# Moving weight loads behind the first heads, halving four kinds of steps, and merging all engine orders anew in a two-layer decoder kernel

## The reference, cut to what matters

```python
x = ln(x + L0_attn(x))             # 16 heads of 16, rotary on q and k, softmax, projection + bias
x = ln(x + L0_xattn(x, ctx, ctx))  # mLSTM-like mixer: 8 heads of 32, q = x, k = v = ctx
                                   # gates from [x, ctx, ctx]; cumsum of log sigmoid, running max,
                                   # D = exp(F_i - F_j + i_j - max); C = q k^T * D / sqrt(32)
                                   # C v / max(|sum C|, exp(-max)), then a norm over each head's 32
x = ln(x + L0_ffn(x))              # int8-like activations, ternary weights:
                                   # h = relu(x Wg)^2 * (x Wu); out = quant(h) Wd
x = ln(x + L1_attn(x))             # 16 heads, no rotary
x = ln(x + L1_xattn(x, ctx, ctx))  # q from x, k and v from ctx, 16 heads, biases
x = ln(x + L1_ffn(x))              # relu(x W1 + b1) W2 + b2
```

## Time and profile before

| | before |
|---|---|
| median of 3 runs | 1883.49 us |
| the profiled execution | 1880.68 us |
| its span, first to last instruction | 1878.8 us |
| TensorE busy | 1595.6 us (85%) |
| VectorE busy | 1189.6 us (63%) |
| ScalarE busy | 965.7 us (51%) |
| GpSimd busy | 222.2 us (12%) |
| mean granted TensorE clock | 0.927 of full |

### The profile page before, as it was taken

How to read it: one execution, slowest core, us unless ns; L and a number is a source line. 1 busy time by engine, 2 the same in 40 slices (tenths; PEclk the granted TensorE clock), 3 DMA queues, 4 the chain that set the end, 5 groups by cost and what they waited for, 6 DMA issues and landing times.

```text
span 1878.8 us, 31464 instructions
## 1 busy us (share of the span) xinstructions
PE 1595.6 (85%) x12530; PEld 1019.0 (54%) x12546; DVE 1189.6 (63%) x2038; ACT 965.7 (51%) x1684; POOL 222.2 (12%) x201
## 2 busy tenths in 40 slices
PE   6388887888998878889999888789999987779888
PEld 4145554555665545455566445456556654546556
DVE  4866778546347777755645875865645677775452
ACT  2067464544554564545465565454556456544643
POOL 5101110010112110101011101100111100100000
PEclk9599998999999998899999988799999989979999
DMA  7600111213110102123111111031320120111200
GB/s 227 214 2 1 40 60 60 91 41 96 57 57 19 67 1 80 60 71 94 42 58 57 46 40 60 21 102 49 96 67 23 46 80 6 60 60 64 81 26 12
DMA packets 116610, 114.34 MB, mean 61 GB/s; under 512 B 10610, under 2 KB 102386, under 8 KB 116466
## 3 DMA queue, kind: packets, MB, share of 16 engines
q1 hardware_dynamic: 116466, 112.33, 19.0%
HBM read 68.91 MB, written 42.99 MB: 60 GB/s over the span
## 4 chain that ended last, share of the span: by engine, by line
PE 62%; DVE 18%; ACT 10%; issue 4%; DMA 3%; SPq 3%; DVEq 0%; ACTq 0%
PE psum L679 9%; PE psum L789 9%; PE psum L672 6%; PE psum L924 6%; PE psum L916 6%; DVE nm L1154 5%; ACT PB L985 4%; PE psum L773 3%; PE psum L754 3%; PE psum L666 3%; PE psum L800 3%; DMA QK<-heads_dram 3%; PE psum L856 2%; PE psum L713 2%; PE psum L868 2%
## 5 line engine op out<-in xcount | busy, mean ns | idle before, releaser
L1154 DVE TENSOR_REDUCE nm<-psum 128x4 f16<-128x1024 f32 x384 | 451.6, 1222 | 152.4 <-PE psum L754 151.5
L985 ACT ACTIVATE PB<-psum 128x1024 f32<-128x1024 f32 x384 | 382.8, 1025 | 205.3 <-PE psum L789 111.8
L1327 POOL TENSOR_TENSOR XO<-XO,row_b 128x512 f32<-128x512 f32 x80 | 102.2, 1280 | 1338.8 <-ACT XT L955 1321.8
L789 PE MATMUL psum<-PB,V 128*32 128x256 f32 x3072 | 226.4, 416 | 14.3 <-ACT PB L985 10.7
L754 PE MATMUL psum<-QK 48*128 48x256 f16 x1536 | 145.4, 291 | 70.5 <-DMA QK<-heads_dram 29.7
L773 PE MATMUL psum<-QK 49*128 49x256 f16 x1536 | 148.2, 292 | 48.6 <-ACT PB L985 22.2
L789 PEld LDWEIGHTS psum<-PB,V 128*32 128x32 f32 x3072 | 88.1, 116 | 98.9 <-issue 48.7
L754 PEld LDWEIGHTS psum<-QK 48*128 48x128 f16 x1536 | 56.5, 97 | 149.7 <-issue 64.8
L773 PEld LDWEIGHTS psum<-QK 49*128 49x128 f16 x1536 | 54.0, 97 | 150.1 <-issue 62.1
L916 PE MATMUL psum<-XT,W 128*128 128x256 f32 x512 | 123.2, 392 | 2.0 <-ACT XT L955 1.6
L924 PE MATMUL psum<-W,PB 128*128 128x256 f32 x512 | 117.7, 383 | 1.4 <-ACT PB L1068 1.3
(11 more groups left out here) (157 smaller groups left out, 2576.1 us busy)
## 6 DMA issues: line engine op xcount, KB each, us to landing
QK<-heads_dram SPq DMA_DIRECT2D x96, 512.0 KB, 4.0
heads_dram<-U SPq DMA_DIRECT2D x288, 128.0 KB, 1.9
XO<-in_x SPq DMA_DIRECT2D x16, 256.0 KB, 2.8
Y<-in_ctx SPq DMA_DIRECT2D x16, 256.0 KB, 3.1
out<-XO SPq DMA_DIRECT2D x16, 256.0 KB, 5.0
W<-in_w SPq DMA_DIRECT2D x2, 1024.0 KB, 9.5
QK<-GN SPq DMA_DIRECT2D x96, 4.0 KB
W<-in_w_gate SPq DMA_DIRECT2D x1, 1024.0 KB, 8.9
```

Source lines behind the costliest of these rows:

```text
L789: ins = pe.matmul(b[SLOT * j:SLOT * j + SLOT, at:at + TOK], value(L, t, PAIRS * e + u, HEADS, HD, SLOT), src, start=(t == 0), stop=(t == T ...
L985: act.activation(PB[L][:, unit % PBUF, :], b[:, 0:1024], ACT.Exp, scale=HD ** -0.5)\
L1154: dve.tensor_reduce(nm[L][:, :, :, unit].rearrange("p t e -> p e t"), b[:, 0:1024].rearrange("p (e t k) -> p e t k", e=2, t=TT), AX.X, ALU ...
L1327: pool.tensor_tensor(stream(L, it), stream(L, it), row_b[:, occ:occ + 1, :].to_broadcast([P, TT, DIM]), ALU.add).then_inc(xb_ready[L], 1)
```

## The change

- The one-time loads are regrouped. `first` keeps constants, inputs, q/k/v weights, the raw feed-forward weights and, as one DMA instead of seven, the bias rows, then the weights to be permuted. All other loads become `weights` 0 to 4; 0 to 3 wait until the stacked operands of lane 0, 1, 2, 3 have landed, and 4 until all ternary weights are made. The four DMAs that fill the constant slots of `heads_dram` are issued by ScalarE.
- TensorE no longer waits for all of GpSimd's memsets at the start; the steps that need them do.
- `R` moves from `U` to `KS` (the half of `QK` for keys), the staged weights to `U` of lanes 2 and 3, the raw down weights to `PB` of lane 3. The ternary weights are made in the order down, gate, up, and only the down weights come before lane 3's rotary.
- `rope` and `qk` of attentions 0 and 1 become two steps each, of one bank and 512 columns instead of two banks and 1024, and so do `stack` and its DMAs. `gateup` becomes `gate` and `up`. `mixnorm` becomes `mixnorm`, `mixvar` and `mixscale`. The work inside is the same.
- `TURNS` and `PLACES` are new throughout. A table `IDLE` with 1905 digits, all zero, is new as well: `claim` would issue extra matmuls by it, and with zeros it issues none.

```diff
-    "quant": "dve pe act", "gateup": "pe act dve", "hT": "pe act", "down": "pe dve act", "up1": "pe act",
+    "quant": "dve pe act", "gate": "pe act", "up": "pe dve", "hT": "pe act", "down": "pe dve act", "up1": "pe act",
...
-WIDTH = {"ctx": 1, "xT": 1, "rope": 2, "qk": 2, "v": 1, "max": 2, "negmax": 1, "exp": 2, "pv": 1, "heads": 2, "oT": 1,
+WIDTH = {"ctx": 1, "xT": 1, "rope": 1, "qk": 1, "v": 1, "max": 2, "negmax": 1, "exp": 2, "pv": 1, "heads": 2, "oT": 1,
...
-        steps = [("first", 0), ("first", 1), ("permute", 0), ("first", 2), ("masks", 0), ("sums", 0), ("scales", 0),
-                 ("ternary", 0), ("ternary", 1), ("weights", 0), ("ternary", 2), ("weights", 1), ("weights", 2), ("weights", 3)]
+        steps = [("first", 0), ("permute", 0), ("sums", 0), ("scales", 0), ("ternary", 2), ("ternary", 0), ("ternary", 1),
+                 ("weights", 0), ("masks", 0), ("weights", 1), ("weights", 2), ("weights", 3), ("weights", 4)]
...
     "pe": (
-        "0002012331223311304210000000033330333322000113000200022002220323013330310333111331022130032322302222"
+        "0003001122311222303310422110000033000222022222111211111233013333330000301000222200222023022033033230"
...
-        R = [v[:, :, :].rearrange("p g t -> p (g t)") for v in U]
+        R = [v.rearrange("p u t -> p (u t)").bitcast(F32) for v in KS]
...
+            def weights(unit):
+
+                if unit < LANES:
+                    sp.wait_ge(stacked[unit], 32)
...
                 elif name == "qk":
-                    j_of = (0, 1) if occ < 2 else (unit,)
+                    j = unit
                     sp.wait_ge(hi_ready[L], it * HI_STEPS + QK_AT[occ, unit])
...
                 elif name == "stack":
                     if (it, occ) == (0, 0):
                         sp.wait_ge(slots_set, 16 * LANES)
-                        if L == 3:
-                            sp.wait_ge(ternary, TERNARY.index("bounded2") + 1)
                     sp.wait_ge(part_out[L], it * OUT_STEPS + OUT_AT[occ, unit])
...
             pe.wait_ge(cst_loaded, 16)
-            pe.wait_ge(set_pool, N_POOL)
+            pe.wait_ge(ident_set, 2)
...
+            act.wait_ge(set_pool, 2)
+            load(slots_set, *[(heads_dram[L][:, :, 3].rearrange("j e r u t -> r (j e) (u t)"), last_rows) for L in range(LANES)])
+            act.wait_ge(set_pool, 4 + 2 * LANES)
```

More of the change, by code:

```diff
@@ L68, in attention @@
             add("xb", a + 1)
-            add("qk", a, 0)
-            add("stack", a, 0)
+            for j in range(2 if a == 1 else 1):
+                add("qk", a, j)
+                add("stack", a, j)
         if a == 1:
@@ L105, in lane_steps @@
     add("mixnorm")
+    add("mixvar")
+    add("mixscale")
     add("mixout")
@@ L109, in lane_steps @@
     for t in range(TT):
-        add("gateup", 0, t)
+        add("gate", 0, t)
+        add("up", 0, t)
     for t in range(TT):
@@ L127, in lane_steps @@
         add("down1", 0, t)
-    add("rope", 0, 0, 1)
-    add("qk", 0, 0, 1)
-    add("stack", 0, 0, 1)
+    for t in range(TT):
+        add("rope", 0, t, 1)
+    for j in range(2):
+        add("qk", 0, j, 1)
+        add("stack", 0, j, 1)
     add("norm", 5)
@@ L296 @@
 SCALED = ("r0", "r1", "r2", "mean", "inverse", "gate2", "gate2up")
-TERNARY = tuple(f"{what}{w}" for w in range(3) for what in ("scaled", "whole", "bounded"))
+TERNARY = tuple(f"{what}{w}" for w in (2, 0, 1) for what in ("scaled", "whole", "bounded"))
 def decoder_kernel(nc, x, ctx, consts, w_qkv0, w_proj0, w_gates, b_gates, w_gate, w_up, w_down,
@@ L607, in _ @@
                 if name == "first":
-                    with nc.allow_non_contiguous_dma(reason="columns of biases, once"):
-                        first(unit)
+                    first()
                 elif name == "weights":
@@ L1135, in _ @@
                     if occ < 2:
[L1136 to L1137 removed]
+                        hi, lo = (flat2(parts[L][:, n, unit]) for n in range(2))
+                        dve.tensor_tensor(lo, b[:, 0:512], hi, ALU.subtract).then_inc(lo_ready[L], 1)
                     else:
```

356 lines of the change are left out of this document (193 added, 163 removed).

## The result

| | kernel before | changed kernel |
|---|---|---|
| median | 1881.02 us (4 runs, 1878.37 to 1884.3) | 1832.97 us (4 runs, 1831.73 to 1834.83) |
| ratio to before, 95% interval | | 0.9745 [0.9722, 0.9767] |
| span of the profiled execution | 1878.8 us | 1830.3 us |
| mean granted clock of TensorE | 0.927 | 0.949 |

The change gains 48 us. The forecast was 1874 (1845 to 1902): the sign was right, the size far off, and the time fell outside the range.

What follows compares the result with a forecast made beforehand. TensorE was taken as the limit from 110 us on, but not before, where VectorE was busier and stacked heads came late. 1880.7 - 13.6 (start) + 2.4 (halves) + 0 (stacks) + 4 (orders) = 1873.5, so 1874 us, range 1845 to 1902.

Steps and rivals of the forecast that it cites:

- Start: Up to lane 0's first heads: the new start order gains 13.6 us, bounds 7 and 24.6.
- the block of maxima: At the start on VectorE: 32 maxima run in one block from about 50 us, ending at 88 us.
- VectorE's first `max`: At the start on VectorE: the first maximum comes at about 50 us (terms given as 49.7) instead of 74.6.
- the start is given back: Rival, at the start: maxima rows behind projection loads delay exponentials some 7 us; 1881 us, chance 0.17.
- Halves: Rotary and heads of attentions 0 and 1: halved steps cost 2.4 us, bounds 0 and 15.7.
- VectorE's busy time: Sign for the whole run: VectorE is busy near 1200 us if the forecast is right.
- SyncE's stack halves: Stacks read in halves on SyncE: about 61 us more standing, nearly all hidden; cost 0, up to 15 us.
- the Trainium skill's rule of about 2 us fixed per DMA: Halved stacks: two rounds make lane start-ups about 2 us longer each, 64 us over 32 before hiding; weighed against the change.
- New orders: Engine orders behind the start: cost 4 us, bounds -25 and +30, the large unknown.
- lanes run closer together, so phases rich in maxima meet: Behind the start: lanes 0 and 1 stand 81 to 86 us apart, before 131 to 137, raising VectorE's excess.
- Bunched lanes: Rival, behind the start: where several lanes' maxima meet, VectorE bounds and TensorE's clock falls; 1898 us, chance 0.23.
- The finer steps fill TensorE: Rival, on TensorE: one-bank claims find room sooner, recovering 22 us of idle time; 1852 us, chance 0.20.

Runs made afterwards that it cites:

- e0: Changed kernel with orders kept on TensorE, VectorE, ScalarE and GpSimd; PSUM banks chosen anew, some SyncE loads and stores change places: 1834.62 us.
- e1: Changed kernel's code and first 112 us, then the order of the kernel before with finer steps side by side: 1900.3 us.
- e10: Changed kernel, but SyncE sends both halves' parts of attentions 0 and 1, waits once, then reads both stacks: 1849.9 us.
- e4: Changed kernel with the first half of each rotary and heads (attentions 0 and 1) put off to right ahead of the second: 1928.94 us.
- e11: e4 with the stacks of both halves joined on SyncE: 1880.01 us.
- e2: Kernel before with its whole steps and own first 110 us, then the changed kernel's order on all engines: 1945.7 us.
- e7: Changed kernel: maxima rows and lane 3's stack before loads, lanes 0 and 2 exponentials among maxima, masks before two ternary sets: 1851.28 us.
- e8: Changed kernel with 48 other steps, drawn at random behind 115 us, put off by 1.6 us on all their engines: 1878.41 us.
- e3: Changed kernel with lanes 3, 2 and 1 put off by 8, 28 and 55 us between 120 and 520 us, orders merged anew: 2350.13 us.
- e14: Changed kernel, SyncE only: bias rows ahead of raw weights, lane 3's second stack and maxima rows ahead of projection loads: 1828.87 us.
- e17: Changed kernel with e14's moves, 140 idle matmuls where TensorE waited, and one ahead of each of 16 early maxima steps: 1831.55 us.
- e13: Changed kernel with SyncE issuing mask, projection and bias loads right behind the first loads, waiting for no stack: 1841.3 us.

## Why the forecast was wrong, point by point

- **Start: 13.6 forecast, 9.5 measured** as work done by 110 us, within its bounds (7 to 24.6), and nothing of it kept: at 200 us of work the changed kernel is 2.9 us behind. The forecast carried the lead at lane 0's first heads to the end of the run, which failed. `row_b` came 3.5 us later than assumed (GpSimd begins at 29.54 us, not 26.0); the block of maxima began 6.5 us late and had three gaps, so it ended at 97.7, not 88. Lane 0's heads start at 111.0 us, the upper end of my 100 to 111, and at 114.9 in e0. Two sums were off by under 1 us: the terms for VectorE's first `max` add to 49.0 us, not 49.7, and an end of 111 us leaves 8 us of gain, not 7. The rival "the start is given back" described this place rightly (rows behind the loads; its 7 us were 4), and more was given back than it had.
- **Halves: 2.4 us forecast.** e1 gives 2.0 us for them side by side in the old order. That doesn't contradict it, but single profiles don't tell 2 us from none. VectorE's busy time fell from 1189.6 to 1171.6 us, where near 1200 was forecast.
- **SyncE's stack halves: 0, up to 15.** Joined, they are 17 us slower in this order (e10), so in it the halving costs nothing. Above I weighed the Trainium skill's rule of about 2 us fixed per DMA ("DMA: Bandwidth & Descriptors", section "Anatomy of one DMA — SWDGE (gpsimd) path"), by which 32 start-ups would each be 2 us longer. The section is about DMAs that GpSimd issues, and SyncE issues these. Where both halves are ready at once the size is near it: e4 less e11, 49 us over 32 start-ups, is 1.5 us each. In the changed order it doesn't decide; that the first half's round lies under the second half's heads there is argued from the order.
- **New orders: +4 us forecast; this is the step that failed.** They gain about 39 us by the cuts in time (19.0 between 110 and 1413 us, 17.5 at the end, 2.6 of busy time), and 51 at equal work, where the changed kernel spends 1542.6 us behind 200 us of work and the kernel before 1593.8. Two arguments of mine were wrong. First, "lanes run closer together, so phases rich in maxima meet" was counted as a cost alone. VectorE's maxima wait 42 us less for TensorE, and TensorE's idle time between 110 and 1700 us fell from 207.6 to 184.3. Second, I gave no thought to the end. Lanes 1 and 2 were 57 and 26 us nearer to lane 0 at its last sequence, so less was left to do with fewer lanes in flight: the four lanes end within 64 us instead of 135. The mean of the four ends moves by 1822.5 - 1799.75 = 22.75 us, the last by 48. The closer lanes follow from the orders I had counted (81 to 86 us of work between lanes 0 and 1 against 131 to 137).
- **Bunched lanes (1898 us)** started from the same closeness of lanes and had the sign wrong. **The finer steps fill TensorE (1852 us)** was nearest in time. Whether it was right in part isn't shown: in the old order the finer steps gained nothing (e1), and e2 lacks a fitted order.

What is shown: old order and finer steps together have no gain (e1); new order and whole steps have none (e2); both together have 48 us. So order and finer steps together carry the gain, and the start doesn't. Runs in the new order idle 46 to 59 us in the last stretch, from lane 0's last first-attention heads on (e4, e7, e8, e10, whatever was disturbed elsewhere), e1 in the old one 65.9, e2 (new order, whole steps) 63.2. That lane distance is the cause there is argued from this and the table above; e3 could not isolate it, and e2 speaks against distance alone. Its lanes are close (by the same count the fourth sequence's heads start at 1507, 1567, 1600 and 1620 us, and the lanes end within 64 us), and yet it idles nearly as long as e1:

```profile
1507.00:1949.70 442.70, 379.45 (x2970) 246.44 (x2966) 266.37 (x496) 227.84 (x409) 40.71 (x38) 0.94 0.15 46
```

So close lanes leave less work for the last stretch (368 us busy in the changed kernel and 379 in e2, against 399 before), but not by themselves less idle time in it. It stays open whether an order fitted anew to whole steps would do as well. That needs a search, which these runs are not. It also stays open how the 19.0 us divide among rotary, heads, gate/up and mixer, since the controls cost as much as each undoing.

## What to carry to other kernels

When an order is merged anew, look at where the streams end, not only at how full each stretch is: with the same pace of the first stream, the time follows the last one, and the distance between streams can be counted in the order before anything runs. Before crediting an early lead, look whether it still stands further on at equal work done. Before crediting a loss to the part that was undone, disturb as many other steps by as much: in a fitted order that alone cost 35 to 45 us here. Put side by side, the finer steps gained nothing here; what the order puts between their halves is where a gain could come from.

## What the runs showed of the hardware

- TensorE's clock at the start rose to the 2.4 GHz level at 99 us in the changed kernel and at 110 in e0, which has the same order on TensorE. So a single run doesn't say what a start's order does to the clock. In e14 it rose at 107 us and in e7, which takes exponentials forward under the maxima, at 120; those exponentials and `pv` ran at the 1.2 GHz level. Idle matmuls ahead of 16 maxima (e17) left the granted clock at 0.50 from 80 to 100 us, with TensorE busy 9.38 and 9.26 of 10 us.
- SyncE is held for the length of an issue. In the changed kernel's start eight W_o loads take 5.4 us of issue (0.67 each, row at 69.19), and in e13 the loads took 30 us where I had taken 24.
- Casts are cheaper without GpSimd beside them. Two casts of 512 columns took 4.58 us beside rotary and take 0.75 now; a multiplication of 128x1 took 1.85 us beside it, the next 0.16:

```profile
45.97 1.85 DVE L1155 TENSOR_TENSOR w_k<-w_scale 128x1 f32<-128x1 f32 x1
47.86 0.16 DVE L1157 TENSOR_TENSOR w_k<-w_k,w_scale 128x1 f32<-128x1 f32 x1
...
105.25 0.75 DVE L1144 CAST sel<-XO 128x512 bf16<-128x512 f32 x2
```

The Trainium skill says both ("SBUF — State Buffer", section "Who interferes with whom"): casts in two-port modes and `tensor_tensor` with two SBUF inputs are shut out while GpSimd holds the shared port. The trace agrees.
